# Turning two states at once in every other slot, and moving the update gate's last product behind the next aggregation

## Time and profile before

| | us |
|---|---|
| median of 3 runs | 771.02 |
| lowest and highest | 769.65 to 773.0 |
| the profiled execution itself | 769.01 |
| its span, first to last instruction | 767.1 |
| PE busy | 751.2 (98%) |
| PEld busy | 630.1 (82%) |
| DVE busy | 624.6 (81%) |
| ACT busy | 513.7 (67%) |
| POOL busy | 166.2 (22%) |

### The profile page before, as it was taken

The page is one execution under the profiler, slowest core; times in us unless marked ns, Lnnn a source line. Parts: engine busy times, 40 slices in busy tenths (PEclk is TensorE's granted clock), DMA queues, the critical chain, the costliest instruction groups (busy, mean ns, idle before and its releaser), DMA issues.

```text
span 767.1 us, 11992 instructions
## 1 busy us (share of the span) xinstructions
PE 751.2 (98%) x3788; PEld 630.1 (82%) x3788; DVE 624.6 (81%) x1447; ACT 513.7 (67%) x1072; POOL 166.2 (22%) x314
## 2 busy tenths in 40 slices
PE   8999999999999999999999999999999999899996
PEld 7888788888888888888888888888887887789885
DVE  5899998888888788877777777887999998785663
ACT  4799877666667766666666666666587857875444
POOL 1778420000000000000000000000123257764334
PEclk9999999999999999999999999999999999999999
DMA  7500000000030001000000000000000000000112
GB/s 226 204 1 2 1 1 1 1 1 1 0 117 1 1 1 56 1 0 1 1 1 0 0 0 0 0 0 2 1 1 1 1 1 1 3 14 28 56 56 83
DMA packets 9895, 16.60 MB, mean 22 GB/s; under 512 B 2929, under 2 KB 4465, under 8 KB 9201
## 3 DMA queue, kind: packets, MB, share of 16 engines
q1 hardware_dynamic: 9840, 15.94, 6.1%
HBM read 8.59 MB, written 5.24 MB: 18 GB/s over the span
## 4 chain that ended last, share of the span: by engine, by line
PE 78%; DVE 9%; ACT 7%; POOL 2%; issue 2%; DMA 1%; SPq 0%; DVEq 0%; ACTq 0%
PE agg_ps L971 12%; PE agg_ps L973 12%; PE agg_ps L972 12%; PE gate_ps L907 7%; PE gate_ps L909 6%; PE gate_ps L908 6%; PE cand_ps L907 4%; PE cand_ps L909 4%; PE cand_ps L908 4%; PE turn_ps L1010 4%; PE gate_ps L914 2%; PE cand_ps L914 2%; DVE stats L810 2%; ACT res L428 2%; ACT feat L505 1%
## 5 line engine op out<-in xcount | busy, mean ns | idle before, releaser
L971 PE MATMUL agg_ps<-adj_hi,nat_hi 128*128 128x512 f32 x384 | 152.1, 396 | 0.0
L973 PE MATMUL agg_ps<-adj_hi,nat_lo 128*128 128x512 f32 x384 | 150.1, 391 | 0.0
L972 PE MATMUL agg_ps<-adj_lo,nat_hi 128*128 128x512 f32 x384 | 149.6, 390 | 0.0
L629 POOL TENSOR_SCALAR shift<-mean_var 128x4 f32<-128x4 f32 x64 | 25.6, 400 | 427.1 <-DVE mean_var L814 424.8
L767 DVE TENSOR_TENSOR agg_lo<-agg_ps,agg_hi 128x512 fp32r<-128x512 f32 x80 | 55.2, 690 | 65.0 <-ACT agg_hi L457 65.0
L490 ACT ACTIVATE reset_hi<-gate_r 128x512 fp32r<-128x512 f32 x80 | 50.6, 633 | 83.1 <-DVE gate_r L784 83.1
L973 PEld LDWEIGHTS agg_ps<-adj_hi,nat_lo 128*128 128x128 f32 x384 | 72.1, 188 | 16.2
L972 PEld LDWEIGHTS agg_ps<-adj_lo,nat_hi 128*128 128x128 f32 x384 | 72.2, 188 | 15.6
L971 PEld LDWEIGHTS agg_ps<-adj_hi,nat_hi 128*128 128x128 f32 x384 | 72.1, 188 | 15.4 <-DVE adj_lo L833 0.3
L474 ACT ACTIVATE gate_r<-gate_ps,bias 128x512 f32<-128x512 f32 x80 | 55.2, 690 | 43.5 <-PE gate_ps L909 43.5
L457 ACT ACTIVATE agg_hi<-agg_ps 128x512 fp32r<-128x512 f32 x80 | 48.7, 608 | 45.3 <-PE agg_ps L973 45.3
(11 more groups left out here) (181 smaller groups left out, 1794.2 us busy)
## 6 DMA issues: line engine op xcount, KB each, us to landing
res<-in_x SPq DMA_DIRECT2D x16, 256.0 KB, 5.3
out<-res SPq DMA_DIRECT2D x16, 256.0 KB, 2.0
rows<-in_adj SPq DMA_DIRECT2D x4, 256.0 KB, 4.0
adj_hi<-eye_hi SPq DMA_DIRECT2D x1, 1024.0 KB, 9.6
adj_lo<-eye_lo SPq DMA_DIRECT2D x1, 1024.0 KB, 11.5
later<-in_adj SPq DMA_DIRECT2D x1, 1024.0 KB, 6.5
mix_rows<-mix SPq DMA_DIRECT2D x1, 1024.0 KB, 8.0
later<-mix_rows SPq DMA_DIRECT2D x1, 1024.0 KB, 4.9
```

The lines of the kernel that those rows point to most:

```text
L971: pe.matmul(ps, nat_hi[:, b, k, :], m_hi[:, k, :], start=(k == 0), stop=False)
L972: pe.matmul(ps, nat_hi[:, b, k, :], m_lo[:, k, :], start=False, stop=False)
L973: last = pe.matmul(ps, nat_lo[:, b, k, :], m_hi[:, k, :], start=False, stop=(k == T - 1))
```

## The change

`states_at(s)` is new: in an even slot it names the units s-5 and s-4, in an odd slot none. Turns, ACT's `nat_hi` and DVE's `nat_lo` follow it. W_ZR of unit s-2 is now issued in slot s, after the aggregation and ahead of U_CAND. On ACT the update gate's sigmoid moves from the head of the slot to the place between `agg_hi` and tanh, and `agg_hi` now waits for W_ZR of unit s-2 (which reads the buffer that it overwrites), where it waited for the reset gate's product.

```diff
+def states_at(s):
+    return [u for u in (s - STATE_LAG - 1, s - STATE_LAG) if is_inner(u)] if s % 2 == 0 else []
 def turns_at(s):
     found = []
-    if is_inner(s - STATE_LAG):
-        found.append(("state", s - STATE_LAG))
+    found += [("state", u) for u in states_at(s)]
...
 ACT:
             def slot(s, ahead):
-                u = s - 2
-                if is_step(u):
-                    act.wait_ge(z_done, ahead(u - B + 1))
-                    if u >= B + 2:
-                        act.wait_ge(move_made, ahead(u - B - 1))
-                    act.activation(gate_z[:, u % 2, :], gate_ps[u % 2][:, :], ACT.Sigmoid,
-                                   bias=bias[:, B_Z:B_Z + 1]).then_inc(z_made, 1)
...
                     act.wait_ge(agg_done, ahead(s + 1))
-                    if s >= 2:
+                    if is_step(s - 2):
+                        act.wait_ge(z_done, ahead(s - 2 - B + 1))
+                    elif s >= 2:
                         act.wait_ge(gate_done, ahead(s - 1))
                     act.activation((agg_hi if is_step(s) else agg_all)[:, s % 2, :], agg_ps[s % 2][:, :],
                                    ACT.Copy).then_inc(agg_hi_made, 1)
                 u = s - 2
                 if is_step(u):
+                    act.wait_ge(z_done, ahead(u - B + 1))
+                    if u >= B + 2:
+                        act.wait_ge(move_made, ahead(u - B - 1))
+                    act.activation(gate_z[:, u % 2, :], gate_ps[u % 2][:, :], ACT.Sigmoid,
+                                   bias=bias[:, B_Z:B_Z + 1]).then_inc(z_made, 1)
                     act.wait_ge(cand_done, ahead(u - B + 1))
...
-                u = s - STATE_LAG
-                if is_inner(u):
+                for u in states_at(s):
                     k = TURN_NO["state", u]
...
 DVE:
-                u = s - STATE_LAG
-                if is_inner(u):
+                for u in states_at(s):
                     dve.wait_ge(state_hi_made, ahead(u - B + 1))
...
 TensorE:
                 u = s - 2
                 if is_step(u):
+                    pe.wait_ge(r_made, ahead(u - B + 1))
+                    product(gate_ps[u % 2][:, :], W_ZR, agg_hi[:, u % 2, :], agg_lo[:, u % 2, :], False,
+                            True).then_inc(z_done, 1)
                     pe.wait_ge(reset_lo_made, ahead(u - B + 1))
...
-                if is_step(u):
-                    pe.wait_ge(r_made, ahead(u - B + 1))
-                    product(gate, W_ZR, *parts, False, True).then_inc(z_done, 1)
```

## The result

The changed kernel takes 805.46 us (median of 6 runs, 802.59 to 808.82), the kernel before 769.54 (6 runs, 769.19 to 773.0). The ratio is 1.046, 95% interval 1.0447 to 1.0478: 35.9 us slower. Forecast were 796.9, range 790 to 807. Direction and range held; the time is 8.6 us above the likeliest case. That nearness is partly luck: the forecast was added to a median of 771.02 for the kernel before, which over six runs is 769.54. The change itself was forecast at 25.9 us and measures 35.9, so it is 10.0 us short. The profiled execution took 805.93 us, its span 804.2.

A forecast was written before the change was run, and what follows sets the result against it. TensorE was taken to set the pace in slots 23 to 96. Terms 21.6 + 4.0 + 1.2 + 0.5 + 1.3 - 1.5 - 1.2 gave 25.9 us more, a median of 796.9 us, range 790 to 807.

The forecast's parts named there:

- the gains: Savings from fewer transpose groups, 1.5 us, and from W_ZR's vanished waits, 1.2 us; 2.7 us together.
- The bank waits: Slots 22, 24, 26, 30, 32, 44, 46: third turn waits for DVE's `nat_lo` of the first state; 21.6 us.
- The late load of U_CAND: After 25 odd slots without a turn, U_CAND's weight load comes 0.28 us late, losing 0.16 each; 4.0 us.
- the loaded slots: Slots 17 to 22, 38 to 42 and 85 to 97, busy on ACT or DVE: 1.2, 0.5 and 1.3 us lost.
- Fewer groups: Slots 20 to 84: 40 groups of turns instead of 65, 0.06 us saved for each; 1.5 us.
- W_ZR's own waits: W_ZR follows the reset gate's sigmoid by a slot, so its weight-load waits in three places go; 1.2 us won.
- the tail: Slots 85 to 97: later tanh makes some five U_CAND loads late, layer-2 seeds' wait included; 1.3 us, 0 to 4.
- The clock: Rival: TensorE's granted clock falls to half in the new waits; 810 us, range 807 to 820, chance 0.05.
- My own sign of being wrong: One of three signs: granted clock leaving 1.00 between 100 and 700 us.
- The price of 13 us: Work after each of the seven waits running at half clock, 1.9 us times seven.
- Other side: Rival, not slower: third turn finds its bank already read, only gains stand; 768.3 us plus U_CAND's cost, chance 0.04.

The follow-up runs named there:

- clear_swap: pair_clear with U_CAND issued behind U_GATE, 0.68 us later in the slot; 769.05 us, ratio 0.9998 to the kernel before.
- pair_clear: The changed kernel, but states turned one by one next to the seven even slots that hold another turn; 775.67 us, ratio 1.0080 to the kernel before.
- fill: The changed kernel with 12 added matmuls that nothing reads ahead of the third turn in the seven slots; 798.25 us, ratio 1.0367 to the kernel before.
- z_only: The kernel before with only the move of W_ZR, one state still turned in each slot; 770.34 us, ratio 1.0011.
- pair_only: The kernel before with two states turned in each even slot, W_ZR left at the end of its slot; 801.85 us, ratio 1.041.
- two_left: pair_clear, but slots 44 and 46 turn two states beside the l2 turn again; 785.56 us, ratio 1.0216 to the kernel before.
- full_swap: The changed kernel with its seven three-turn slots and U_CAND issued behind U_GATE; 801.51 us, ratio 1.043 to the kernel before.

## Why the prediction held, and where it was short

Four runs on top of each other give the whole sum, in medians: before 769.5; clear_swap 769.05 (-0.5); late loads of U_CAND, pair_clear - clear_swap, 775.67 - 769.05 = 6.6; bank waits, fill - pair_clear, 798.25 - 775.67 = 22.6; low clock, changed kernel - fill, 805.46 - 798.25 = 7.2. Together 35.9. Against the forecast of 25.9 the clock is 7.2 us more, the gains came out 2.2 smaller (0.5 instead of 2.7), the bank waits 1.0 larger and the late loads 0.4 smaller.

- **The bank waits** (21.6 forecast) measured 22.6, 3.2 for each of seven. That figure holds three late loads too, in slots 24, 26 and 32, which pair_clear avoids; without them, at 0.27 each, it is 21.8. Place, cause and size held: the idle is 2.8 to 3.1 us of PE and ends with DVE's `nat_lo`, and pair_clear removes it by nothing but the place of the states.
- **The late load of U_CAND** (4.0, and 3.0 for the loaded slots) measured 6.6 in total, for the 22 such slots of pair_clear and the loaded ones. That the sum came out so near is partly luck. Beside the loaded slots the load is late behind exactly the 25 slots that were named, but the single loss was 0.27 instead of 0.16 us, since the chain was 0.06 us longer than computed and the distance between matmuls recovers only over the next ones. In exchange the loaded slots 17 to 21 cost nothing: there the changed kernel was 1.2 us faster, of which 0.69 is W_ZR's product leaving slot 17 (it comes in again in slot 97) and 0.43 the transposes of slot 21, which slot 22 now carries.
- **Fewer groups** (1.5 forecast) held where it can be read: a pair of slots in the loop takes 13.15 us in clear_swap and 13.21 before (means over slots 48 to 83), 0.06 less for one group less, as computed.
- **W_ZR's own waits** (1.2 won) are gone in slots 88 and 93, 0.3 and 0.4 us, but slots 89, 92 and 94 (0.7 together) and above all 97 (1.0, of which 0.7 is the product from slot 17) take it back, as z_only shows on its own: 0.9 us slower. I had put the tail into one figure of 1.3.
- **The clock** is the step that failed. I gave its fall in the new waits 0.05 and left it out of the sum and of the range. It fell after 3 of 7 waits in the profiled run, and the runs show 7.2 us, of which 5.8 in the profiles stand behind those three waits. My own sign of being wrong, a granted clock that leaves 1.00 between 100 and 700 us, came true; that the time still lies in the range is luck. The price of 13 us was for a fall after all seven, 1.9 each, and 1.9 is what each of the three cost on average; a fall after some of the waits was not among the rivals. The rows bracketed the wait, a gap of 1.86 us that kept the clock and one of 3.5 us that lost it, and 3.0 lies nearer to the second; 0.05 had no ground in them. The Trainium skill's rule ("TensorE: Matmul & The Clock Gate", "Why this matters for your kernels"), that idle gaps between bursts bring the half rate, is borne out by this case: 2.8 to 3.1 us of idle did so after some waits and not after others of the same execution. What decides between them is not shown.
- **Other side.** No sign of it: A's `nat_lo` ends about 2.8 us or more after the eighth transpose in all seven slots.

## What to carry to other kernels

Before two uses of a two-deep ring are put into the same slot, list everything else that takes a buffer from that ring there: a third user waits for the first one's whole read-out, and on an engine with no slack that is lost time. A wait on TensorE of about 3 us had two prices here, the wait and the chance that the work behind it runs at the low clock; put both into the sum. When a block is moved to shorten one wait, recompute the next operand of the same chain: here the move was covered only while every slot carried its own transposes, and putting U_CAND three matmuls later restored that cover.

## What the runs showed of the hardware

- A matmul of 128x512 starts 0.227 us after the one before at granted clock 1.00 and 0.43 at 0.50.
- TensorE idle (PE) was followed by granted clock 0.50 after 1 of 7 waits of 2.6 to 2.8 us (pair_only), after 3 of 7 of 2.8 to 3.1 us (the changed kernel), after 2 of 2 of 3.1 us (two_left), after 3 of 7 of 3.3 to 3.5 us (full_swap), and after none once 12 matmuls filled the wait (fill).
- The shorter gaps do not set a safe length: 1.86 us in slot 104 of the kernel before kept the clock, but 1.76 us ahead of slot 0 in the changed kernel and 1.74 in pair_only were followed by 0.50, and 1.74 in fill was not.
- The three falls in the changed kernel cost 1.5 to 2.8 us each, 5.8 together.
- A weight load that comes 0.34 or 0.35 us late costs 0.23 us over the next two matmuls, 0.27 in all (the means of the pairs), and starts 0.05 us after its operand is written.
- A filler that nothing reads made the kernel faster (84 matmuls, 7.2 us in the medians, 5.8 of it seen in the slots of the waits).
